# A transformer block in one launch: the keys' transfers and their copy move ahead of the attention's, and in even steps the next keys are turned earlier and the early key sums are added ahead of h's rounding

## The reference, cut to what matters

```python
q = jax.nn.relu(split_heads(xn @ Wq)) + 1e-3      # 16 heads of 64
k = jax.nn.relu(split_heads(xn @ Wk)) + 1e-3
v = split_heads(xn @ Wv)
context = cumsum(einsum('bhnd,bhne->bhnde', k, v), axis=2)
D_inv = 1.0 / einsum('bhnd,bhnd->bhn', cumsum(k, axis=2), q)
attn = einsum('bhnd,bhnde,bhn->bhne', q, context, D_inv)
x = x + merge_heads(attn) @ Wo + bo
gate, y = fp4_linear(xn2, w_gate), fp4_linear(xn2, w_up)   # 256 -> 704
out = x + fp4_linear(silu(gate) * y, w_down)               # 704 -> 256
```

## Time and profile before

| | |
|---|---|
| median of 3 runs | 1524.68 us (1521.96 to 1528.65) |
| the profiled execution | 1526.87 us, span of its instructions 1525.1 us |
| TensorE (PE) busy, share of the span | 1463.2 us, 96% |
| VectorE (DVE) | 1147.0 us, 75% |
| ScalarE (ACT) | 642.6 us, 42% |
| GpSimd (POOL) | 723.8 us, 47% |
| granted TensorE clock, mean | 0.998 of full speed |
| share of the span in which its queue's packets kept the 16 DMA engines | 39.4% |

### The profile page before, as it was taken

One profiled execution on the slowest core, in us unless ns is written; L12 is line 12 of the kernel. 1 busy time (PEld: TensorE's weight loads), 2 busy tenths in 40 slices (PEclk: granted clock), 3 DMA queues, 4 the chain that ended last, 5 costly groups with the idle time before them and its releaser, 6 DMA issues.

```text
span 1525.1 us, 54703 instructions
## 1 busy us (share of the span) xinstructions
PE 1463.2 (96%) x23324; PEld 1369.0 (90%) x23324; DVE 1147.0 (75%) x2363; ACT 642.6 (42%) x1124; POOL 723.8 (47%) x822
## 2 busy tenths in 40 slices
PE   8889999999999999999999999999999999999998
PEld 7878999889899899998999989898998989999888
DVE  8786778777777777778777777777777776778767
ACT  5433443344443443444344453444443343443333
POOL 4313554444554545554544554444554444554443
PEclk9999999999999999999999999999999999999999
DMA  5101344354453444344354453445344354453410
GB/s 168 34 2 43 88 126 140 95 157 115 122 154 102 133 130 138 115 140 133 102 158 122 127 142 114 126 125 150 110 132 135 101 156 121 117 154 105 123 50 15
DMA packets 188880, 176.24 MB, mean 116 GB/s; under 512 B 16224, under 2 KB 174944, under 8 KB 188640
## 3 DMA queue, kind: packets, MB, share of 16 engines
q1 hardware_dynamic: 188640, 172.75, 39.4%
HBM read 89.59 MB, written 83.10 MB: 113 GB/s over the span
## 4 chain that ended last, share of the span: by engine, by line
PE 37%; DMA 14%; issue 13%; DVE 10%; SPq 10%; POOL 9%; ACT 2%; DVEq 0%; POOLq 0%; ACTq 0%
PE bank L652 28%; DMA hq_away<-hq_blocks 5%; DMA attn_away<-probs 4%; DMA key_stage<-keys_away 4%; SPq L568 3%; SPq L585 3%; PE bank L853 2%; PE bank L785 2%; POOL hqT_lo L1589 2%; SPq L599 2%; POOL attnT_lo L1577 2%; DVE hq_blocks L2024 2%; PE bank L819 2%; DVE attn L1947 2%; POOL hq L1565 2%
## 5 line engine op out<-in xcount | busy, mean ns | idle before, releaser
L652 PE MATMUL bank<-xT_hi,wqk_hi 128*128 128x256 f32 x1024 | 212.0, 288 | 5.2 <-ACT qkT L1173 2.0
L652 PE MATMUL bank<-xT_hi,wqk_lo 128*128 128x256 f32 x1024 | 203.9, 280 | 0.0
L652 PE MATMUL bank<-xT_lo,wqk_hi 128*128 128x256 f32 x1024 | 203.8, 280 | 0.0
L1577 POOL TENSOR_TENSOR attnT_lo<-attn,attnT_hi 128x1024 fp32r<-128x1024 f32 x58 | 155.5, 2681 | 73.9 <-ACT attnT_hi L1260 73.8
L1173 ACT ACTIVATE qkT<-bank 128x512 f32<-128x512 f32 x256 | 148.6, 592 | 88.3 <-PE bank L652 87.1
L1637 POOL TENSOR_SCALAR qkT<-qkT 128x512 f32<-128x512 f32 x256 | 158.5, 633 | 39.7 <-ACT qkT L1173 38.8
L652 PEld LDWEIGHTS bank<-xT_hi,wqk_hi 128*128 128x128 f32 x1024 | 157.7, 189 | 9.5 <-issue 6.1
L1616 POOL TENSOR_TENSOR xq<-x_scaled,x_scale 128x256 f32<-128x256 f32 x64 | 49.8, 778 | 227.6 <-DVE x_scaled L1803 227.5
L652 PEld LDWEIGHTS bank<-xT_hi,wqk_lo 128*128 128x128 f32 x1024 | 157.1, 189 | 0.0
L652 PEld LDWEIGHTS bank<-xT_lo,wqk_hi 128*128 128x128 f32 x1024 | 156.7, 188 | 0.0
L1310 ACT ACTIVATE silu<-bank 128x352 f32<-128x352 f32 x128 | 58.6, 458 | 232.4 <-PE bank L652 232.1
(11 more groups left out here) (220 smaller groups left out, 3796.6 us busy)
## 6 DMA issues: line engine op xcount, KB each, us to landing
attn<-attn_away SPq DMA_DIRECT2D x232, 128.0 KB, 3.1
hq_away<-hq_blocks SPq DMA_DIRECT2D x58, 384.0 KB, 3.1
hq<-hq_away SPq DMA_DIRECT2D x232, 96.0 KB, 2.3
keys_away<-key_stage SPq DMA_DIRECT2D x41, 512.0 KB, 3.2
key_stage<-keys_away SPq DMA_DIRECT2D x164, 128.0 KB, 3.4
attn_away<-probs SPq DMA_DIRECT2D x58, 256.0 KB, 2.7
attn_away<-probs SPq DMA_DIRECT2D x116, 128.0 KB, 2.7
x_in<-in_L_attn_x SPq DMA_DIRECT2D x32, 256.0 KB, 2.9
```

Source lines behind the costliest of these rows:

```text
L652: at = pe.matmul(dst, lhs_at(kt), rhs_at(kt), start=first and kt == 0, stop=last and kt == k_tiles - 1)
L1577: pool.tensor_tensor(by_raw_attn(attnT_lo), attn_raw, by_raw_attn(attnT_hi).bitcast(F32), ALU.subtract).then_inc(attnT_ready, 2)
```

## The change

SyncE issues the keys' fetch ahead of the attention's sending in the first step of a sequence, and in odd steps sends the keys ahead of the attention and fetches them in the same order. ScalarE copies the keys ahead of the attention and of h's square in even steps with sent keys. VectorE turns the next keys (c = 0) right behind the masks, ahead of `low_xq`, and in even steps with sent keys adds the early sums ahead of `round_h`. Odd steps of ScalarE and VectorE, TensorE and POOL are as they were.

```diff
@@ SyncE: step, c % 2 == 0
                     if c == 0 and g + 1 in SENT_KEYS:
                         send_keys(g + 1)
+                        fetch_keys(g + 1)
                     if g in SENT_ATTN:
                         send_attn(g)
-                    if c == 0 and g + 1 in SENT_KEYS:
-                        fetch_keys(g + 1)
-                    if g in SENT_ATTN:
                         fetch_attn(g)
@@ SyncE: step, c % 2 == 1, behind h's
+                    if g + 1 in SENT_KEYS:
+                        send_keys(g + 1)
                     if g in SENT_ATTN:
                         send_attn(g)
                     if g + 1 in SENT_KEYS:
-                        send_keys(g + 1)
+                        fetch_keys(g + 1)
                     if g in SENT_ATTN:
                         fetch_attn(g)
-                    if g + 1 in SENT_KEYS:
-                        fetch_keys(g + 1)
@@ ScalarE: even_step
                 high_x(c, u + 1)
+                if g in SENT_KEYS:
+                    keys_by_tokens(b, c)
                 if g - 1 in SENT_ATTN:
                     high_sent_attn(g - 1)
                 if g > WARM:
                     square_h(g - 3)
-                keys_by_tokens(b, c)
+                if g not in SENT_KEYS:
+                    keys_by_tokens(b, c)
                 high_xq(g - 2)
@@ VectorE: even_step
                 if not is_late(g - 1):
                     variance(g - 1)
-                low_xq(g - 2)
-                round_h(g - 3)
-                add_early(g)
                 if c == 0 and g + 1 in SENT_KEYS:
                     block_keys(g + 1)
+                low_xq(g - 2)
+                if g in SENT_KEYS:
+                    add_early(g)
+                    round_h(g - 3)
+                else:
+                    round_h(g - 3)
+                    add_early(g)
                 if not is_late(g - 1):
                     begin_x(g - 1)
```

## The result

The changed kernel took 1514.28 us (median of 6 runs, 1507.38 to 1517.63), the kernel before 1523.68 beside it: ratio 0.9934, interval 0.9913 to 0.9955, a gain of 9.4 us. The direction was forecast, and the time lies inside the range (1496 to 1516), but under half of the 22 us came. The profiled execution took 1515.2 us, its span 1513.5, against 1525.1 before.

What follows compares the result with a forecast made beforehand. TensorE was taken as the bound, with 33.8 us idle in the steady part, 25.0 of it waits the change moves. 12.8 + 2.7 - 3 + 7.8 + 1.7 + 3 - 3 = 22.0 us gave a median of 1503 us, range 1496 to 1516.

Steps and rivals of the forecast that it cites:

- 12.8 + 2.7 - 3: First steps: 12.8 us of early-sum waits and 2.7 of key waits go, some 3 us of waiting stay.
- what waits hide: TensorE's busy time: a wait hides 0.3 us more in modelled ends; sixteen give 4.8, taken as 3 us gain.
- 7.8 us: Second steps: all of TensorE's wait for late keys goes, as the keys are turned, sent and fetched earlier.
- The same edit without the turning: 1.7 us, all of it.: Third steps: TensorE's waits for keys, three in number and 1.7 us together, vanish entirely.
- VectorE loses 0.4 us: First steps: `normalize` comes 0.4 us later against TensorE, at no cost; without cover, 5.6 us over 14 steps.
- New stalls: TensorE's unexplained stops on L853 partly show up in first steps once these run through: 0 to 5 us, taken as 3.
- (a): Rival: landings trade unevenly, attention comes 2.6 us later, first steps gain nothing; about 1515 us, chance 0.12.
- (b): Rival: 8 to 10 us given back as first-step stops or through `normalize`; 1512 us, chance 0.17 shared with (d).
- (c): Rival: slower, attention's landing slips 4 us or more behind a late key turning in odd steps; about 1548 us, chance 0.07.
- (d): Rival: queue order without effect, keys and attention land together at 685.57; 1510 us, chance 0.17 shared with (b).
- L785's two rows from 12.2 to under 1: Sign in the profile after: TensorE's waits of `early_keys` fall from 12.2 us to under 1.
- the last one: Sign: TensorE's busy time between steps 8 and 60 comes within 15 us of the stretch, else the forecast is wrong.

Runs made afterwards that it cites:

- experiment 3: Changed kernel with ScalarE's copy order in third steps and SyncE's order of second steps as before: 1508.18 us, 0.9914 to the kernel before.
- the two doses: Changed kernel plus unused VectorE statistics in first steps: behind the attention's turning 1515.18 us, 0.994; ahead of it 1524.56 us, 0.9994.
- the two attempts at the reverse: h's additions behind the attention's turning in first steps: atop the new bank, earlier variance and earlier second silu 1497.63 us; in the changed kernel 1544.63 us.
- experiment 7: Kernel before with only VectorE's early sums moved ahead of h's rounding in even steps with sent keys: 1537.14 us, 1.0087.
- experiment 6: Changed kernel with VectorE's early sums again behind h's grid additions, all else as changed: 1544.85 us, 1.0147 to the kernel before.

## Why the prediction was right, and where it failed

**First steps: right.** The sum had 12.8 + 2.7 - 3, and 3 more for what waits hide; 16.9 came. The wait for the early sum went from 13.2 us to nothing, where up to 5 were allowed; what is left there is 2.1 to 3.5 us on L817, of another kind (below). TensorE's busy time in first steps fell by 3.7 us (198.7 to 195.0, worked out from the traces), so the term for what waits hide was of the right size. The attention's copy stood where it was put in step 28 (2.51 us into the step, forecast 2.59). The keys landed sooner than thought, in time for a copy at 681.47 and not 683.8.

**Second steps: mostly right.** ScalarE no longer stands for keys, and SyncE issues the sending at 685.49 (forecast near 686). ScalarE's idle time for the keys' landing there went from 46.7 us to nothing. Of 7.8 us 5.5 came.

**Third steps: the step that failed.** The prediction put it as "The same edit without the turning: 1.7 us, all of it." It was a loss of 6.4, so 8 of the 9 us that are missing (22 less the 12.8 of the spans). I looked only for who waits for keys there. The edit gives the attention the later landing and puts it behind the key copy, as in first steps; xq is copied behind both, and in third steps `early_keys` itself takes the bank that xq must leave. In first steps I had followed exactly this chain, with a price for each part of it; in third steps I copied the wait row. Changing the bank takes third steps to 188.0 us, and six profiles with it have 188.0 to 191.8: by the traces the bank is shown as the cause; the times of the one direct pair show 2 us of it. The new row on L817 in first steps is the same kind of wait, for xq's bank 4: each of its 17 waits in the four profiles ends 0.10 us after `low_xq` does, so "issue" is not what it waits for. A plan that frees it there was not tried.

**"VectorE loses 0.4 us. Its step is not full ... so this costs nothing": wrong as an argument.** The room in VectorE's step lies behind the attention's turning. Relative to its step's start that turning moved forward by 0.48 us on average (10.05 to 9.57 us into the step; 0.57 to 0.64 in the repeats), and TensorE's first step got shorter by 1.1 to 1.2. The rest, about 0.6, became lateness of the attention in the second step, and of what VectorE does there: 0.3 to 0.4 us at the attention's copy, 0.5 to 0.6 at POOL's low part and at `normalize`; third steps, even with the old order of transfers, get keys and attention about 1 us later into the step (experiment 3). That a lateness at this place is paid in full is shown by the two doses; how much of the missing 2.3 us of second steps and of third steps' loss it makes is not, since the two attempts at the reverse gave no clear answer.

**New stalls: 3 forecast, about 3 found, and they can be named.** The "issue" rows on L853 and L652 (now L851 and L650) made 11.9 us before and 15.2, 11.5, 18.2 and 16.2 in the four profiles of the changed kernel, 3.4 more on average. Most of them stand at the same place in nearly every profile: after 2095, 3973, 4976, 6854, 9735, 10738, 13619 and further matmul records. Some are new, after 12616 (step 34, three of four profiles) and 15497 (step 42, two of four). The distances between all these places are whole multiples of 125.25 matmuls, while two sequences have 2888, no multiple of it: they go by a count of instructions, not by the product. The profile's queue of instructions moved blocks of 16 KB:

```profile
q8 instruction: 186, 3.05, 0.9%
```

Set beside the times of these 186 transfers in the traces, every one of the 74 stops in the five profiles ends 1.20 to 1.60 us after such a transfer has ended, while the waits on L785 before end 0.6 to 11.4 us after one. So the stops are late fetches of instructions, though the view calls them "issue". The prediction names the Trainium skill ("Runtime: NRT & Kernel Launch", section "Instruction fetch mechanics"), which calls these fetches mostly hidden. By count the traces agree, 13 to 17 of 186 are late; but their 11.5 to 18.2 us are no zero, and the row in the prediction was the better guide.

The reasoning behind the term was right as well: where a wait goes, such a stop can come up, as with the early sum alone (experiment 7), which has three new ones in first steps, 3.8 us. And it works the other way: in third steps the changed kernel has 3.2 to 7.3 us of them on L851, the six profiles with the other bank have none. In step 18 the fetch starts 1.4 us after `early_keys` in the changed kernel and 0.65 us ahead of it with the other bank; that the wait for the bank holds the fetch back is likely, not shown.

**The rivals.** By their times (a), 1515, and (b), 1512, both lie beside the measured 1514.28, and that is luck. (a) wanted first steps to gain nothing, and they gained all they could. (b) had `normalize` and more stalls; the late turning of the attention is near to the first, but most of the loss lay in third steps' bank. (c) and (d) fell: in step 28 keys and attention did trade landings, and the attention's came where it was put.

**The marks.** Of those named beforehand, "L785's two rows from 12.2 to under 1" failed (3.9, and 1.6 to 7.6 in the repeats), and so did the last one: 22.8 us of the stretch were idle, not under 15. The growth of the "issue" stops by about 3 us held.

**The range.** With all three terms at their bounds the sum runs from 13 to 29 us, which is 1496 to 1512 and not 1497 to 1510. And that the time lies inside the range of 1496 to 1516 says little for the forecast, since the range took in (a) and (b). By the medians 12.6 us of the 22 are missing, 9.2 by the spans.

## What to carry to other kernels

A row of waits says who is late for whom today; when an edit is used in several kinds of steps, follow the whole chain in each kind, down to the buffers and banks that the moved work holds, because the delayed partner (here the attention, and xq behind it) meets other owners there. A step that "isn't full" has room only behind the point that someone waits for: find the instruction that starts the next transfer and count the slack there; a short useless instruction put once ahead of it and once behind it measures just that. Two parts of a reordering may each lose alone (here 14 and 21 us) and still belong to a whole that gains. And stops of TensorE that an "issue" row shows can be told apart: those that keep the same distances in matmuls from one kernel to the next, and that end behind a transfer of the instruction queue, are late fetches, and a changed order can move them but has no wait there to remove.

## What the runs showed of the hardware

**A half-clock stretch behind a long wait.** In step 22 of the changed kernel TensorE waited 2.94 us on L783; windows (us, busy PE, PEld, DVE, ACT, POOL, clock, DMA, GB/s):

```profile
546.00:549.70 3.70, 0.76 (x13) 0.35 (x15) 0.42 (x1) 2.79 (x5) 1.59 (x1) 1.00 0.02 6
549.70:553.10 3.40, 3.40 (x137) 3.40 (x136) 2.39 (x3) 0.19 (x1) 0.79 (x2) 0.51 0.02 5
```

TensorE was busy 0.76 us of 3.70, and then worked 3.4 us at the lower of its two levels, 1.2 GHz: some 1.7 us on top of the wait. The changed kernel's profiles have 2 to 4 such stretches, that of before 2, both ahead of step 8; so late landings cost more than their wait now and then. In experiment 6, with waits of up to 2.1 us in each first step, there are five in first steps alone.

**VectorE and POOL hold each other up.** Step 49 of the changed kernel:

```profile
1155.20 3.04 POOL L1578 TENSOR_TENSOR attnT_lo<-attn,attnT_hi 128x1024 fp32r<-128x1024 f32 x1
```

```profile
1156.84 2.15 DVE L1802 SCALAR_TENSOR_TENSOR h_scaled<-h_square,h_scaled 128x704 f32<-128x704 bf16 x1 [0.86 <-ACT h_square L1313]
1159.03 0.89 DVE L1804 SCALAR_TENSOR_TENSOR h_scaled<-h_square,h_scaled 128x704 f32<-128x704 bf16 x1
```

The first grid addition takes 2.15 us while POOL makes the attention's low part, the second, of the same size, 0.89 once POOL is done. Over the whole trace the first one takes 0.88 us (median) in 20 cases with POOL idle and 2.14 in 25 beside this instruction of POOL; beside another one of POOL's, L1617, it takes 0.89, so not every instruction of POOL does this. POOL's takes from 2.36 to 3.06 us. It is one more link by which a late attention delays VectorE in second steps.
